# 68 instead of 56 weighted blocks built beside the attention of a four-layer graph network

## What is computed

```python
q = q_all[dst]
k = k_all[src] + e
v = v_all[src] + e
alpha = (q * k).sum(-1) * scale
amax = jax.ops.segment_max(alpha, dst, num_segments=N)
ex = jnp.exp(alpha - amax[dst])
denom = jax.ops.segment_sum(ex, dst, num_segments=N)
w = ex / denom[dst]
agg = jax.ops.segment_sum(v * w[:, None], dst, num_segments=N)
...
msgs = edge_values[:, None] * X[src]
AX = jax.ops.segment_sum(msgs, dst, num_segments=X.shape[0])
return jnp.einsum('nd,od->no', AX, W) + b
```

## Time and profile before

| what | value |
|---|---|
| three runs | 5624.51, 5627.88, 5636.4 us, median 5627.88 us |
| the profiled execution | 5615.62 us, span 5614.0 us |
| PE, DVE busy | 4809.8 us (86%), 3803.6 us (68%) |
| ACT, POOL busy | 2156.4 us (38%), 2084.1 us (37%) |
| mean granted TensorE clock | 0.935 of full speed |

### The profile page before, as it was taken

One profiled execution on the slowest core, in us unless ns is written; L12 is line 12 of the kernel. 1 busy time (PEld: TensorE's weight loads), 2 busy tenths in 40 slices (PEclk: granted clock), 3 DMA queues, 4 the chain that ended last, 5 costly groups with the idle time before them and its releaser, 6 DMA issues.

```text
span 5614.0 us, 102733 instructions
## 1 busy us (share of the span) xinstructions
PE 4809.8 (86%) x38297; PEld 3472.2 (62%) x38297; DVE 3803.6 (68%) x6119; ACT 2156.4 (38%) x3962; POOL 2084.1 (37%) x2152
## 2 busy tenths in 40 slices
PE   1299999948989888889888988859999998689997
PEld 0276666626777777777777777535555543456665
DVE  4888888757777777777777777479999976420001
ACT  0166666545555555555555555422222200000001
POOL 4122210007777777777777777200000000001110
PEclk6699999979999999999999999979999999699998
DMA  7256665427777777777777877649999999156664
GB/s 217 70 183 208 209 204 197 165 104 199 219 218 217 216 215 213 214 208 218 211 214 207 217 205 217 177 141 293 286 291 290 289 276 252 53 185 206 203 204 119
DMA packets 1256468, 1154.88 MB, mean 206 GB/s; under 512 B 468015, under 2 KB 1149860, under 8 KB 1207060
## 3 DMA queue, kind: packets, MB, share of 16 engines
q1 hardware_dynamic: 1129992, 802.56, 49.2%
q0 software_dynamic: 87488, 151.98, 11.8%
q10 hardware_dynamic: 38495, 193.76, 9.9%
HBM read 691.89 MB, written 468.81 MB: 207 GB/s over the span
## 4 chain that ended last, share of the span: by engine, by line
PE 47%; SPq 21%; DVE 9%; POOL 9%; issue 7%; DMA 4%; ACT 1%; DVEq 0%; POOLq 0%; ACTq 0%
PE psum L1385 46%; SPq L624 5%; POOL G L835 4%; SPq L627 4%; POOL H L835 4%; DVE R L858 4%; SPq L621 3%; DMA H<-local_dst_pairs 3%; SPq L632 2%; SPq L505 2%; DVE H L858 1%; SPq L483 1%; SPq L613 1%; DVE ACC L858 1%; POOL R L786 1%
## 5 line engine op out<-in xcount | busy, mean ns | idle before, releaser
L1385 PE MATMUL psum<-R,HT 128*128 128x384 bf16 x6076 | 1084.2, 326 | 59.8 <-DVEq L1374 59.8
L1703 ACT ACTIVATE HT<-psum 98x512 f32<-98x512 f32 (+2 forms) x1527 | 978.9, 679 | 381.6 <-PE psum L1385 307.9
L1385 PE MATMUL psum<-R 128*128 128x98 bf16 (+3 forms) x6858 | 982.6, 281 | 70.1 <-DVE R L858 27.7
L1703 ACT ACTIVATE H<-psum 128x512 f32<-128x512 f32 (+1 forms) x752 | 446.7, 597 | 1508.3 <-PE psum L1607 796.4
L835 POOL DMA_INDIRECT G<-gather_table,cols_pc x908 | 867.8, 956 | 420.0 <-issue 270.7
L835 POOL DMA_INDIRECT H<-gather_table,cols_pc x896 | 856.3, 956 | 295.0 <-issue 264.9
L1385 PEld LDWEIGHTS psum<-R,HT 128*128 128x128 bf16 x6076 | 566.7, 97 | 383.6 <-DVEq L1374 60.1
L1385 PE MATMUL psum<-R,ACC 128*98 128x128 bf16 x10752 | 784.6, 222 | 0.0
L1385 PEld LDWEIGHTS psum<-R,ACC 128*98 128x98 bf16 x10752 | 746.8, 126 | 0.2
L858 DVE TENSOR_TENSOR HT<-HT,psum 128x512 f32<-128x512 f32 (+1 forms) x949 | 607.6, 653 | 153.1 <-PE psum L1385 149.5
L1385 PEld LDWEIGHTS psum<-R 128*128 128x128 bf16 (+1 forms) x6858 | 568.8, 111 | 226.0 <-issue 36.8
(11 more groups left out here) (237 smaller groups left out, 5947.2 us busy)
## 6 DMA issues: line engine op xcount, KB each, us to landing
weighted_blocks<-HT ACTq DMA_DIRECT2D x224, 784.0 KB
adjacency_blocks<-HT SPq DMA_DIRECT2D x74, 1568.0 KB, 5.7
ACC<-weighted_blocks SPq DMA_DIRECT2D x74, 1568.0 KB, 12.9
R<-weighted_blocks SPq DMA_DIRECT2D x74, 1568.0 KB, 12.4
HT<-adjacency_blocks SPq DMA_DIRECT2D x50, 1568.0 KB, 6.5
H<-local_dst_pairs SPq DMA_DIRECT2D x113, 512.0 KB
weighted_blocks<-H SPq DMA_DIRECT2D x72, 784.0 KB
R<-attr_parts SPq DMA_DIRECT2D x451, 99.0 KB
```

The costliest lines, as they stand in the source:

```text
L1385: return nc.tensor.matmul(o, lhs_t, rhs, start=start, stop=stop)
L1703: return nc.scalar.activation(o, a, f, **kw)
```

## The change

NPL falls from 18 blocks to 6, so NPRE rises from 56 to 68. Beside the attention PRE_CH rises from 224 chunks to 272 and the builds PRE_N from 896 to 1088. The 549 rounds (ROUNDS = 2 x 272 + 5) are dealt over the same 456 steps by `rounds_of`: 363 steps have one round and 93 have two. A step with two rounds has four builds, of which two stand ahead of the score products and two at the step's end. In the send loop 96 builds are left instead of 288, and they are spread over 66 x 13 = 858 sends instead of 54 x 13 = 702.

```diff
--- before.py
+++ after.py
@@ -73,7 +73,7 @@
     J = 2 * W
     HB = 16
 
-    NPL = NBK // 4
+    NPL = (NBK + 11) // 12 // 2 * 2
     NPRE = NBK - NPL
     PRE_CH = NPRE * 4
     PRE_N = PRE_CH * 4
@@ -509,7 +509,12 @@
         COLS_READY = 16 * (2 + FG)
 
         STEPS = GN + 5
-        assert 2 * STEPS - 5 >= PRE_N
+        ROUNDS = 2 * PRE_CH + 5
+        assert ROUNDS >= STEPS
+
+        def rounds_of(k):
+
+            return range(k * ROUNDS // STEPS, (k + 1) * ROUNDS // STEPS) if 0 <= k < STEPS else range(0)
 
         LATE = NPL * 16
         SENDS = NB * (NPRE - 2)
@@ -670,8 +675,9 @@
                         numbers = load_windows(ENG.SP, k, GR)
                     load_queries(k)
                 g = k - AHEAD
-                if k % 8 == 6 and 2 <= (k + 2) // 8 < NPRE:
-                    load_columns((k + 2) // 8)
+                for v in rounds_of(k):
+                    if v % 8 == 6 and 2 <= (v + 2) // 8 < NPRE:
+                        load_columns((v + 2) // 8)
                 if g in range(GN):
                     if g % GR == 0:
                         places = load_places(g, GR)
@@ -1314,9 +1320,10 @@
                     v.wait_ge(s_min, p + 1)
                     ts(dif[:, p % CH:p % CH + 1], newm[:, p % CH:p % CH + 1], oldm[:, p % CH:p % CH + 1], stay[:, p:p + 1],
                        ALU.subtract, ALU.min).then_inc(s_dif, 1)
-                if k < 2 * PRE_CH:
-                    for j in range(2) if k % 2 == 0 else range(2, 5):
-                        hot_step(k // 2, j)
+                for u in rounds_of(k):
+                    if u < 2 * PRE_CH:
+                        for j in range(2) if u % 2 == 0 else range(2, 5):
+                            hot_step(u // 2, j)
             v.wait_ge(s_acc, GN)
             den = lns[:, 0, :]
             for b, (w0_, n) in enumerate(BLK):
@@ -1606,8 +1613,10 @@
                     for j in range(GR):
                         last_ins = nc.tensor.transpose(bank4(5)[:, j, :], masked[:, (k - 3) % 3, j * P:(j + 1) * P], ident[:, :])
                     last_ins.then_inc(s_et, 1)
-                if 2 * k - 5 in range(PRE_N):
-                    build_weighted(2 * k - 5)
+                beside = [n for u in rounds_of(k) for n in (2 * u - 5, 2 * u - 4)]
+                for n in beside[0:len(beside) // 2]:
+                    if n in range(PRE_N):
+                        build_weighted(n)
                 if k - 1 in range(GN):
 
                     t.wait_ge(s_gt, k)
@@ -1626,8 +1635,9 @@
                     for j in range(GR):
                         last_ins = nc.tensor.transpose(bank4(0)[:, j, :], slot(GR * k + j)[:, 0:F], ident[:, :])
                     last_ins.then_inc(s_t, 1)
-                if 2 * k - 4 in range(PRE_N):
-                    build_weighted(2 * k - 4)
+                for n in beside[len(beside) // 2:]:
+                    if n in range(PRE_N):
+                        build_weighted(n)
             transposes(2, lambda w: ACC[:, w, 0:F], s_agn)
             transposes(3, lambda w: ACC[:, w, F:FX], rows=X1)
             t.wait_ge(s_trc, 4 * NB)
@@ -1855,8 +1865,9 @@
                     if k >= 4:
                         act.wait_ge(s_use, k - 3)
                     activation(ET, bank4(5), ACT.Copy).then_inc(s_etc, 1)
-                if k % 2 == 1 and (k - 5) // 2 in range(PRE_CH):
-                    store_pairs_beside((k - 5) // 2)
+                for u in rounds_of(k - 1):
+                    if u % 2 == 0 and (u - 4) // 2 in range(PRE_CH):
+                        store_pairs_beside((u - 4) // 2)
                 if k - 2 in range(GN):
                     p = k - 2
                     act.wait_ge(s_min, p + 1)
@@ -1864,9 +1875,10 @@
                     activation(e, e, ACT.Exp, bias=newm[:, p % CH:p % CH + 1], scale=-1.0).then_inc(s_exp, 1)
                     act.wait_ge(s_dif, p + 1)
                     activation(corr[:, p % CH:p % CH + 1], dif[:, p % CH:p % CH + 1], ACT.Exp).then_inc(s_c, 1)
-                for n in (2 * k - 6, 2 * k - 5):
-                    if n in range(PRE_N):
-                        copy_weighted(n)
+                for u in rounds_of(k):
+                    for n in (2 * u - 6, 2 * u - 5):
+                        if n in range(PRE_N):
+                            copy_weighted(n)
                 if k in range(GN):
                     act.wait_ge(s_t, k + 1)
                     if k >= 2:
```

## The result

| | before | after |
|---|---|---|
| three runs | 5627.88 us (5624.51 to 5636.4) | 5762.64 us (5753.06 to 5762.66) |
| ratio | | 1.0237 [1.0209, 1.0264] |
| span of the profiled execution | 5614.0 us | 5751.5 us |
| attention, first gather to last stored sum | 2329 us | 2542 us |
| send loop, end of block 0 to end of block 71 | 1035 us | 956 us |

The change makes the kernel 135 us slower; 36 were forecast, and 5762.64 lies above the range. The two stages explain it: +213 us for the attention (forecast +110), -79 us for the send loop (forecast -73 for this stretch), 134 together.

What follows compares the result with a forecast made beforehand. SP's queue, which hardly ever waits, was taken to pace the attention: +101 (stores) +9 (column loads) there, -74 in the send loop, sum +36 us on 5627.9, so 5664 us; range 5585 to 5725.

Steps and rivals of the forecast that it cites:

- 48 x 2.1 = +101: Attention: 48 more stores on ACT's queue each hold up SP's queue by 2.1 us, +101 us (bounds nothing and 119).
- Column loads, +9: Attention: 12 more column loads on SP's queue at 0.58 + 0.14 us each, +9 us (bounds 9 and 18).
- I cost this at zero: Attention: second rounds in 93 steps add nothing, covered by DVE's 391 us of waiting; uncovered, 158 us (PE) or 226 (DVE).
- SP has always been busy with other items by then: Attention: a second round delays the sums that SP waits for by up to 2.4 us, without holding SP up.
- the cover: Attention: the 391 us for which DVE waits for SP's node numbers, 3.5 us every fourth step, hide the second rounds.
- Over all steps PE's own pace becomes 4.68 us: Attention: with 93 second rounds PE alone needs 4.68 us a step, under SP's 5.11 now and 5.35 later.
- the second round binds too: Rival, attention: second rounds lengthen the loop from masks to node numbers, +56 us expected, in all +92, 5720 us; chance 0.15.
- the attention holds its pace: Rival, attention: stores don't slow SP's queue, only transfer time counts; -65 us in all, 5563 us; chance 0.15.
- a share of 23% of DMA time that is free: Attention, rival that it holds its pace: more stores cost only transfer time, of which 23% is free.
- The send loop, -73: Send loop, end of block 0 to block 71: 65 blocks at 13.6 us and 6 at 12.97, 962 us against 1035.

Runs made afterwards that it cites:

- e3: Kernel before, stores beside the attention cut from 8 KB to 512 B a row from the fifth chunk on (output wrong): 0.9946, attention 2286 us.
- e5: Changed kernel, stores beside the attention cut from 8 KB to 512 B a row from the fifth chunk on (output wrong): 0.9984, attention 2396 us.
- e8: Kernel before with one more register read of window numbers on SP's queue every fourth step, kept in the program: 1.0255, attention 2487 us.
- e6: Kernel before with the loads of node numbers issued four groups earlier, ahead of the sums' store: 0.9937, attention 2288 us.
- e7: Changed kernel with the loads of node numbers issued four groups earlier, ahead of the sums' store: 1.0039, attention 2422 us.
- e1: Changed kernel with rounds dealt so that nearly all two-round steps begin with an even round (4 of 93 odd): 1.0232, attention 2514 us.
- e2: Changed kernel with rounds dealt so that 91 of 93 two-round steps begin with an odd round: 1.0267, attention 2554 us.
- e13: Changed kernel with node numbers loaded four groups earlier and two-round steps beginning even: 1.0063, attention 2424 us.
- e17: Changed kernel with two-round steps beginning even and stores of 512 B a row (output wrong), node numbers not moved: 0.9831, attention 2297 us.
- e18: Changed kernel with its own mix of odd and even steps, early node numbers and stores of 512 B a row (output wrong): 0.9989, attention 2393 us.
- e16: Changed kernel with early node numbers, two-round steps beginning even and stores of 512 B a row (output wrong): 0.9835, attention 2306 us.
- e14: Changed kernel with early node numbers and 91 of 93 two-round steps beginning odd: 1.0241, attention 2525 us.
- e9: Changed kernel with early node numbers and two-round steps beginning even: 1.011, beside a kernel before that took 6153.43 us.
- e10: Changed kernel with early node numbers and 91 of 93 two-round steps beginning odd: 1.0563, beside a kernel before that took 6153.43 us.
- e12: Changed kernel with early node numbers, even two-round steps and stores of 512 B a row (output wrong): 0.9971, beside a kernel before at 6153.43 us.
- e15: Version with 62 blocks beside the attention (45 two-round steps, 5 odd) and early node numbers: 1.0029, attention 2375 us.

## Why the prediction was wrong

The direction and the mechanism were right: each store moved beside the attention holds up SP's queue, and the attention follows that queue (e3, e5, e8). The send loop came out as forecast; of the attention's growth the forecast saw half. Too small was what SP's queue would cost, and the second rounds were put at nothing. I added up the duration of every SP instruction within the attention, and split it into a base (each instruction at the lower quartile of its kind), the stretch above it, and idle time. The three make up the attention by construction: they say where SP's time went, not why.

| | base | stretch | idle | attention |
|---|---|---|---|---|
| before | 1589 | 498 | 240 | 2329 |
| after | 1599 | 646 | 294 | 2542 |
| e3, before with small stores | 1582 | 104 | 599 | 2286 |
| e5, after with small stores | 1591 | 123 | 679 | 2396 |
| e6, before with early numbers | 1556 | 502 | 228 | 2288 |
| e7, after with early numbers | 1566 | 609 | 245 | 2422 |

- **"Four steps have two such stores. If all of the stretch is theirs, a store costs 2.1 us", hence 48 x 2.1 = +101.** The mechanism is right, the size is not. Nearly all of the stretch is the stores' (498 against 104 in e3). On the mean a store costs (498 - 104) / 220 = 1.8 us before and (646 - 123) / 268 = 1.95 after. But the stretch grew by 148 us, of which 129 go away with the stores' bytes: 2.7 us for each of 48. A mean was taken for a price at the margin, and this term was undersized by 47 us. Why the added ones are dearer is not shown: in e8 the stretch grows by 31 us with no store added. With early numbers it is 609 - 502 = 107, close to 101.
- **Column loads, +9.** The base grew by 10.
- **"I cost this at zero" (the second rounds): this step failed.** SP's idle time grew by 54 us, which is its wait for DVE's sums (68.9 against 14.5). "SP has always been busy with other items by then" was read from a kernel in which no step was long. Even steps leave most of the wait (50.8 us in e1), odd ones add to it (113.4 in e2), early numbers leave less (22.9 in e7, 16.7 in e13). I read it as the loop over the node numbers, whose double steps with masks take 8.9 us even where they begin even.
- **A second path that the prediction did not have** lies under this one: the build that needs products of its own double step, 3.4 us in 42 steps. It follows from the order of the queues; the cover was counted in each engine's total (391 us of DVE's waiting). In the changed kernel it is nearly hidden (28 us by e1's attention, while the ratios 1.0232 and 1.0237 can't be told apart); with small stores it is the bound (99 us, e5 against e17; 96, e18 against e17).
- **"Over all steps PE's own pace becomes 4.68 us"** holds where double steps begin even: 93 steps of 6.1 and 363 of 4.33 make 4.69 on the mean, and e16 and e17 stay at POOL's floor. So the work itself does cost nothing. With odd steps (e14) it is 5.54 us a step.
- So the terms are 110 as forecast, 47 more stretch, 1 more base and 54 idle: 212 of the 213 us.
- **Rival "the second round binds too" (5720)** was the right one for what was left out. SP did begin to wait, 54 us more, where +56 was expected. The other 43 us up to 5763 are about the 47 us by which the stretch was undersized.
- **Rival "the attention holds its pace"** is out: stores without bytes give 2396 instead of 2542. Its number, a share of 23% of DMA time that is free, said nothing on SP's queue. The Trainium skill, Perfetto Trace Analysis, section "DMA Instruction — HWDGE (DVE, Sync)", lets such an issue's duration include a wait for a descriptor generator that is shared. The runs agree in that an issue is stretched by what another queue has issued. They add that equally many packets with an eighth of q10's bytes stretch it hardly at all; whether the wait is one for the generator they don't show.
- **The send loop, -73**: measured -79. 13.6 us a block was 13.56, and 12.97 for the rest was 12.4.
- **The range** has two slips that change nothing here: 5585 leaves out a third of the first rival's gain of 65 us, not a half, and the upper rival stands at 5720, not 5725.

Undoing one cause in the changed kernel shortens its attention by 146 us (small stores), 120 (early numbers) or 28 (even steps, not seen in the ratio). They overlap, so they don't add up.

What stays open: how early numbers work. Of the 120 us between the changed kernel and e7, idle time gives 49, the stretch 37, and 33 the base, mostly one register load (below). In e6 the same 33 us are most of the 41 gained, so e6 doesn't tell a shorter queue from an earlier load. I read the first two as the loop from masks over sums, SP's store and the node numbers back to masks, which passes each delay on; no run separates them. Also open is why PE was held up in e9 (and, by their times, in e10 to e12).

The best version measured that computes the whole result is e6: 56 blocks as before, and the node numbers early, 0.9937 [0.9914, 0.9959]. With early numbers 62 blocks (1.0029) and 68 (1.0039, 1.0063) are slower than that.

## What to carry to other kernels

Price an item that is added to a queue without waits at its margin and not at the mean of those that are there, and test it by taking its bytes away, not its issue. When steps are doubled, write out for each parity of the first round which operation of the step needs which of the same step; a chain across engines inside one step costs its full length even where each engine's total has room, as soon as no longer path covers it. If undoing a plain cause changes nothing, a second path of the same length may lie under it: take that away first, then try again.

## What the runs showed of the hardware

- A store of 784 KB from ACT's queue stretches the issues on SP's queue by 1.8 to 1.95 us on the mean, and by 2.7 us for each of the 48 that were added (with early numbers 2.2 for each of 48 in e7, 2.7 for each of 24 in e15). With 512 B instead of 8 KB a row, and as many packets, the stretch is nearly gone (646 to 123 us in all).
- The same register load on SP (L505) has a median of 1368 ns in the kernel before, and of 1045 ns in e6, where another instruction stands ahead of it. Over 113 of them that is 36 us; the cause is open. Between 2000 and 3000 us of e6, min/median/max:

```profile
L505 SPq TENSOR_LOAD <-put x49: 1026/1045/4345, 2012.7 to 2982.4; - x49
```

- In one set (e9 to e12) the kernel before took 6153.43 instead of some 5610 us. In e9 PE is idle within single builds, and all of the loss lies in the attention: 3013 us against 2424 in e13, the same kernel, while its send loop, from the second gather to the last, took 972 us against 975. PE's waits in e9 from 1259 to 3900 us (0.5 us in the changed kernel on its own occasion):

```profile
PE psum L1397 <- issue: 455.0, 618, 6.5
```
